# Values of three attentions written token by token to DRAM and read back, in place of a masked copy and transposes

## What is computed

```
q, k, v = split(x @ qkv_w.T + qkv_b)          # x: 64 images, 17 tokens, 192 features
q, k = rms_norm(q), rms_norm(k)                # first block's attention (a0) only
w = softmax(q @ k.T / sqrt(16))                # per image and head: 17 x 17
ctx = w @ v                                    # 12 heads of 16 features
h = h + ctx @ proj_w.T + proj_b
```

## Time and profile before

| | us |
|---|---|
| median of 3 runs | 935.1 |
| lowest and highest run | 934.97, 940.88 |
| profiled execution, its own time | 934.18 |
| span of the profiled execution | 932.1 |
| stage a0, from TensorE's first to last instruction | about 39.5 to 145.7 |
| stage a2 | about 553.7 to 636.2 |
| stage a3 | about 727.2 to 838.4 |

### The profile page before, as it was taken

How to read it: one execution, slowest core, us unless ns; L and a number is a source line. 1 busy time by engine, 2 the same in 40 slices (tenths; PEclk the granted TensorE clock), 3 DMA queues, 4 the chain that set the end, 5 groups by cost and what they waited for, 6 DMA issues and landing times. The chain is left out here.

```text
span 932.1 us, 16890 instructions
## 1 busy us (share of the span) xinstructions
PE 854.9 (92%) x6194; PEld 608.5 (65%) x6195; DVE 447.4 (48%) x903; ACT 387.8 (42%) x857; POOL 186.7 (20%) x207
## 2 busy tenths in 40 slices
PE   6899888999998799999989789999999999999997
PEld 5556656677775467777668466765687566666776
DVE  5566676777744412222268666551104566633111
ACT  2366653453542022333243864554151455532332
POOL 0610003444500134445200012220000000002232
PEclk9999999999988899999999999999999999997999
DMA  8000000000004967112150019000000211102111
GB/s 294 1 2 1 1 2 0 1 2 1 1 2 102 256 182 198 46 51 46 39 164 3 0 45 258 6 2 28 1 1 1 56 50 50 52 19 97 43 51 34
DMA packets 30638, 51.07 MB, mean 55 GB/s; under 512 B 3750, under 2 KB 23752, under 8 KB 30572
## 3 DMA queue, kind: packets, MB, share of 16 engines
q1 hardware_dynamic: 22140, 36.09, 14.0%
q0 software_dynamic: 4416, 9.84, 3.8%
q10 hardware_dynamic: 4016, 4.23, 1.4%
HBM read 43.30 MB, written 6.83 MB: 54 GB/s over the span
## 5 line engine op out<-in xcount | busy, mean ns | idle before, releaser
L79 PE MATMUL banks<-con 128*128 128x512 f32 (+1 forms) x206 | 95.1, 572 | 3.0 <-DVEq L2136 1.4
L1846 PE MATMUL banks<-moe_wu,moe_xf 96*128 x256 | 92.1, 505 | 1.6 <-ACT moe_xf L1954 0.8
L634 PE MATMUL banks<-x,a_wqkv 96*96 96x272 f32 x288 | 74.6, 397 | 0.9 <-PEq L457 0.5
L1846 PEld LDWEIGHTS banks<-moe_wu,moe_xf 96*128 96x128 f32 x256 | 47.5, 195 | 31.4 <-issue 4.8
L944 ACT ACTIVATE a_vt<-banks 102x384 f32<-102x384 f32 x96 | 41.9, 488 | 50.4 <-PE banks L710 50.1
L154 ACT ACTIVATE ln_sq<-x 96x544 f32<-96x544 f32 x32 | 21.1, 658 | 93.2 <-DVE x L146 93.2
L634 PEld LDWEIGHTS banks<-x,a_wqkv 96*96 96x96 f32 x288 | 45.4, 164 | 18.2 <-issue 3.2
L79 PEld LDWEIGHTS banks<-con 128*128 128x128 f32 x206 | 38.4, 202 | 25.9 <-issue 22.4
L2151 DVE TENSOR_TENSOR moe_hid<-banks,moe_gs 128x384 f32<-128x384 f32 x32 | 17.9, 558 | 77.6 <-PE banks L1846 77.6
L710 PE MATMUL banks<-con,a_vx 96*102 96x96 f32 x384 | 42.7, 253 | 7.4 <-ACT a_vt L944 6.1
L2008 POOL DMA_INDIRECT moe_xs<-moe_x_rows,moe_taken x32 | 31.2, 974 | 76.1 <-PE banks L1830 54.2
(11 more groups left out here) (409 smaller groups left out, 1772.2 us busy)
## 6 DMA issues: line engine op xcount, KB each, us to landing
moe_wu<-in_moe_up SPq DMA_DIRECT2D x16, 576.0 KB, 8.9
f_w<-in_f_e SPq DMA_DIRECT2D x10, 576.0 KB, 14.6
moe_wd<-in_moe_down SPq DMA_DIRECT2D x16, 288.0 KB, 9.9
patch_px<-in_patches SPq DMA_DIRECT2D x4, 768.0 KB, 9.4
f_wu<-in_f_up SPq DMA_DIRECT2D x4, 582.0 KB
f_wd<-in_f_down SPq DMA_DIRECT2D x4, 576.0 KB
f_x_rows<-f_xtok ACTq DMA_DIRECT2D x4, 384.0 KB, 3.4
a_wqkv<-in_a_wqkv SPq DMA_DIRECT2D x3, 432.0 KB, 8.3
```

Source lines behind the costliest of these rows:

```text
L79: self.nc.tensor.matmul(self.ps[bank][:, 0:width], self.ident, self.con[:, 0:width], start=True, stop=True)
L634: last = nc.tensor.matmul(ps[2 + m][0:HD, 0:CW], wqkv[:, a, j * D + m * HD:j * D + (m + 1) * HD], chunk(x, c)[:, a], start=a == 0, stop=a ...
L1846: last = nc.tensor.matmul(ps[2 + 2 * p + u][:, 0:BW], xf[0:KU[a], p, a], wu[0:KU[a], bass.ds(e, 1), a, u * BW:(u + 1) * BW].rearrange("p e ...
```

## The change

The values no longer go through the masked copy and the transposes. TensorE projects them token-major (`values`): the tokens are the stationary operand, so that a result has tokens on partitions: two groups of products for 128 tokens by 192 features, and one of the last 32 tokens of the chunk for each half. ScalarE evicts them in two instructions (`take_values`) into `vtok`. SP writes them to DRAM in four transfers (`write_values`) as two planes, one for each half, of 272 rows of 96 features. Then six transfers for each chunk (`read_heads`) read them back, one for each head in a half: 18 partitions (17 keys and one of padding), 32 runs in each (16 images in 2 planes) of 16 features, that is 64 bytes. They land in `vt`, which GpSimd has set to zero before (`vt_zero`), on partitions key * 6 + head. So the order of the 102 columns becomes (key, head) where it was (head, key): `kx`, `p`, the maxima and the sums follow it. `vt` is double by chunk.

For chunk 0, SP issues the reads of heads 0, 2 and 4 and ScalarE those of 1, 3 and 5; for the others SP issues all six. The read of chunk c waits until the writes of its chunk have landed, and from chunk 2 on for the products that still read the buffer. `values` of chunks 0 and 1 run in the stage's opening, those of chunk 2 and 3 at the head of the loop for chunks 0 and 1. The weights loaded ahead are cut in four parts (`load_part`), one issued after each chunk's reads.

```diff
-    def load(self, sp):
-        sp.dma_start(self.gw[:], self.dram["gw"]).then_inc(self.gw_in, 16)
-        for i in range(6):
+    def load_part(self, sp, part):
+        if part == 0:
+            sp.dma_start(self.gw[:], self.dram["gw"]).then_inc(self.gw_in, 16)
+        for i in self.PARTS[part]:
...
+    def load_part(self, sp, part):
+        self.load(sp, range(part, part + 1))
...
+        vtok = sb("vtok", [128, 2, 2 * D + HD])
+        vt_rows = sb("vt", [(N + 1) * HH, 2, 2 * IC, HD])
+        v_rows = nc.dram_tensor(name + "_v_rows", (NC, 2 * CW + 1, HD), F32).ap()
...
+        def read_heads(eng, c, heads):
+            for h in heads:
+                eng.dma_start(vt_rows[h::HH, c % 2, :, h * HW:(h + 1) * HW],
+                              bass.AP(v_rows.tensor, c * (2 * CW + 1) * HD + h * HW, [[HD, N + 1], [N * HD, 2 * IC], [1, HW]])).then_inc(v_in[c % 2], 16)
...
-            for w in ahead:
-                w.load(sp)
+            def write_values(c):
+                rows = v_rows[c, 0:2 * CW].rearrange("(a t) d -> t a d", a=2)
+                for u in range(2):
+                    sp.wait_ge(v_taken, 2 * c + 1)
+                    sp.dma_start(rows[128 * u:128 * (u + 1)], vtok[:, c % 2, u * D:(u + 1) * D].rearrange("p (a d) -> p a d", a=2)).then_inc(v_written, 16)
+                for a in range(2):
+                    sp.wait_ge(v_taken, 2 * c + 2)
+                    sp.dma_start(rows[256:CW, a], vtok[SLOT * (a + 1) - (CW - 256):SLOT * (a + 1), c % 2, 2 * D:2 * D + HD]).then_inc(v_written, 16)
+            def read_values(c):
+                sp.wait_ge(v_written, 64 * (c + 1))
+                if c < 2:
+                    sp.wait_ge(vt_zero, c + 1)
+                else:
+                    sp.wait_ge(ctx_ready, GPC * (c - 1))
+                read_heads(sp, c, range(HH) if c else range(0, HH, 2))
+            sp.wait_ge(vt_zero, 1)
+            sp.dma_start(v_rows[:, 2 * CW:2 * CW + 1].rearrange("c t d -> t c d"), vt_rows[0:1, 0, 0:NC]).then_inc(v_padded, 16)
+            write_values(0)
+            sp.wait_ge(v_padded, 16)
+            read_values(0)
+            for c in range(NC):
+                if c + 1 < NC:
+                    write_values(c + 1)
+                    read_values(c + 1)
+                for w in ahead:
+                    w.load_part(sp, c)
...
-            def project_v(c, m):
-                pe.wait_ge(qk_evicted, NT * c + 2 + m + 1)
-                project(c, 2, v_proj, m)
+            def values(c):
+                if c >= 1:
+                    pe.wait_ge(v_taken, 2 * c)
+                for u in range(2):
+                    for a in range(2):
+                        tokens = chunk(x, c)[:, a, 128 * u:128 * (u + 1)]
+                        nc.tensor.matmul(v_bank[:, u * D:(u + 1) * D], tokens, wqkv[:, a, 2 * D:3 * D], start=a == 0, stop=a == 1)
+                for a in range(2):
+                    tokens = chunk(x, c)[:, a, CW - SLOT:CW]
+                    for m in range(2):
+                        last = nc.tensor.matmul(v_bank[SLOT * m:SLOT * (m + 1), 2 * D:2 * D + HD], tokens,
+                                                wqkv[:, a, 2 * D + m * HD:2 * D + (m + 1) * HD], start=a == 0, stop=a == 1)
+                last.then_inc(v_proj, 1)
...
             def weigh(g):
+                c = g // GPC
                 pe.wait_ge(pt_evicted, g + 1)
-                pe.wait_ge(vt_evicted, (g + 1) * FV)
+                if g % GPC == 0:
+                    pe.wait_ge(v_in[c % 2], 16 * HH * (c // 2 + 1))
...
+            def take_values(c):
+                act.wait_ge(v_proj, c + 1)
+                if c >= 2:
+                    act.wait_ge(v_written, 64 * (c - 1))
+                nc.scalar.activation(vtok[:, c % 2, 0:2 * D], v_bank[:, 0:2 * D], ACT.Copy).then_inc(v_taken, 1)
+                nc.scalar.activation(vtok[0:64, c % 2, 2 * D:2 * D + HD], v_bank[0:64, 2 * D:2 * D + HD], ACT.Copy).then_inc(v_taken, 1)
...
+            act.wait_ge(v_written, 64)
+            act.wait_ge(v_padded, 16)
+            act.wait_ge(vt_zero, 1)
+            read_heads(act, 0, range(1, HH, 2))
...
+            for c in range(2):
+                pool.memset(vt_rows[:, c], 0.0).then_inc(vt_zero, 1)
+                if c == 0 and response is not None:
+                    response.on_pool(pool, 1)
```

More of the change, by code:

```diff
@@ L280, in allocate @@
             self.bg, self.b2 = self.sb("bg", [128, E]), self.sb("b2", [128, E, D])
+    def load_part(self, sp, part):
+        if part == 0:
+            self.load(sp)
     def load(self, sp):
@@ L647, in project_q @@
                     project(c, 0, q_proj, m)
-            def project_v(c, m):
-                pe.wait_ge(qk_evicted, NT * c + 2 + m + 1)
-                project(c, 2, v_proj, m)
+            def values(c):
+                if c in carried:
+                    pe.wait_ge(before.ready, c + 1)
+                if c >= 1:
[10 more added lines that the diff above has]
+                last.then_inc(v_proj, 1)
             def states():
@@ L695, in scores, with turn_inputs @@
                 last.then_inc(scored, 1)
[L697 to L721 removed]
+            def turn_inputs(g):
+                if g == 0:
+                    pe.wait_ge(s_taken, 1)
+                else:
+                    pe.wait_ge(xt_taken, g)
+                for f in range(2):
+                    for a in range(2):
+                        o = (g * GI + 4 * f) * N
+                        last = nc.tensor.transpose(ps[6][0:4 * N, (2 * f + a) * HD:(2 * f + a + 1) * HD],
+                                                   x[:, a, o:o + 4 * N], env.ident[0:HD, 0:HD])
+                last.then_inc(xt_ready, 1)
             def turn_weights(g):
@@ L747, in weigh @@
                                                 pt[:, g % 2, 2 * (i // 4) + a, SLOT * (i % 4):SLOT * (i % 4 + 1)],
-                                                vt[:, g % 2, i, a, :], start=True, stop=True)
+                                                vt[:, c % 2, a, (g % GPC) * GI + i, :], start=True, stop=True)
                 last.then_inc(ctx_ready, 1)
@@ L799, in _ @@
                 pe.wait_ge(wo_in, 32)
+            values(0)
+            if quantum:
                 states()
             project_k(0)
+            values(1)
             for c in carried:
@@ L812, in _ @@
                 head_mean_square(1)
-            for m in range(2):
-                project_v(0, m)
             if rms:
@@ L823, in _ @@
                 more = c + 1 < NC
-                turn_values(2 * c)
+                if quantum:
+                    if c == 0:
+                        pe.wait_ge(s_factor, 1)
+                    turn_inputs(2 * c)
+                if c + 2 < NC:
+                    values(c + 2)
                 if c >= 1:
@@ L857, in _ @@
                     head_mean_square(NT * (c + 1) + 3)
-                if more:
-                    project_v(c + 1, 0)
                 if quantum:
```

145 lines of the change are left out of this document (57 added, 88 removed).

## The result

| | before | after |
|---|---|---|
| median, us | 935.04 | 975.76 |
| lowest and highest run | 934.89, 940.88 | 971.3, 981.56 |
| span of the profiled execution | 932.1 | 969.0 |

What follows compares the result with a forecast made beforehand. TensorE was taken to bound all three attention stages, with SyncE's queue ending a3 after the change. 934.2 - 5.2 - 8.1 + 2.3 + 7.0 = 930.2, with 0.9 to the median: 931 us; range 912 to 950.

Steps and rivals of the forecast that it cites:

- by the same count as above: a0's boundaries, counted like a2's with measured piece lengths kept in the new order: -2.2, -3.1 and -1.9 us.
- a2's -8.1: Stage a2: periods of 16.8 or 15.7 us for 18.68, plus 0.3 us from the opening; 8.1 us shorter.
- a0's -5.2: Stage a0: opening longer, three boundaries shorter without transposes and VectorE's copy; 5.2 us shorter, bounds -2 to -8.
- The opening was forecast at +2.05: a0's opening: values of two chunks before the first scores, few transposes taken out; 2.05 us longer.
- a3's +2.3: End of a3: SyncE's queue with the experts' weights ends after TensorE, hiding its gain; stage 2.3 us longer.
- TensorE alone was forecast at -14.5: a3: TensorE's list shortens by 1.3 in the opening and 3.5, 5 and 5 at boundaries, ending near 824 us.
- SyncE was forecast done 113.6 us into the stage: a3: SyncE issues its last expert weights about 841 us, by 828.3 + 21 r with r = 0.6.
- 17.0 were forecast on top: a3: the first weights are issued later by 11.6 + 9 r us, behind the first two chunks' writes and reads.
- the sum had 1 us: a3, SyncE's queue between weight parts: 1 us in each 1 + 6 r + 1.5 for chunks 2 and 3.
- r: Time of one read of 18 by 32 runs of 64 bytes: 0.6 us, low 0.45, up to 1.2, worst 1.6.
- Rival C: Slower, chance 0.20: reads cost r = 1.2 us, a3 +14.8 and f3 +8; total 945 us, 960 with r = 1.6.
- f3's +7.0: Start of f3: last up weights still occupy one engine, delaying token rows and the first gather; 7.0 us longer.

Runs made afterwards that it cites:

- the stall away: Changed kernel with a2's scaling of x on VectorE moved behind the scaling of the second group's context; 965.5 us, a2 74.3 us.
- the filled and cut version: Changed kernel with idle products sized to the gap, a2's scaling of x late and up weights in transfers of 96 and 1 partitions; 923.9 us, 0.9872 times before.
- the clock held: Changed kernel with a2's scaling late, up weights cut and later chunks' value products moved into the gap as real work; 917.2 us, 0.9787 times before.

## Why the prediction was wrong

By stages the forecast was -5.2, -8.1, +2.3 and +7.0 for a0, a2, a3 and f3, and 0 for the rest; measured were +10.6, -0.3, +13.0, +10.1 and +3.5.

- **The step that failed: the clock had no term in the sum, and a0 and a3 were counted "by the same count as above", from a2.** That count lets the second set of context transposes follow the first after 1.46 or 1.42 us. For a2 it holds (1.45 with the stall away). In a0 the distance was VectorE's chain already before, 3.39, 4.02 and 4.02 us, and in a3 2.91, 3.54 and 3.54. There the half projection did not lengthen TensorE's list but covered a wait. Without it the wait grew from 0.97 to 2.19 and from 1.60 to 2.82 us in a0 and from 0.88 to 2.16 in a3, and behind it the clock was at its lower level for 7 to 20 us. The clock was read from the earlier trace rows (0.98 and 1.00) and taken to stay; no term, no rival and no bound had it, though the 0.98 of a0 was a fall behind such a wait. That the gap brings the fall was shown in both directions, by filling it in the changed kernel and by opening it in the kernel before, though not every gap brings one. Against the filled and cut version a0 lost about 11 us by gap and clock (117.3 and 106.1).
- **The order (key, head).** The prediction asked only whether the copy of the keys gets slower. It took 6.04 us for 6.47, but that is not the new order: with the same order it took 6.51 where VectorE's scaling began in its first half. The sum over strided columns, 0.3 us slower, was never priced. With VectorE's stall and the clock behind it, it took all of a2's gain.
- **a2's -8.1** was right otherwise: -8.5 with the stall away, with periods of 16.8 and 15.7 us as forecast.
- **a0's -5.2.** The opening was forecast at +2.05 and measured at +6.5, of which 2.8 are left at the full clock and in a better order (18.5 against 15.7). With the clock held a0 gains 9.5 (97.2), more than forecast.
- **a3's +2.3**: measured +13.0. TensorE alone was forecast at -14.5 (its terms give 14.8); measured are -9.4 with both limits gone. SyncE was forecast done 113.6 us into the stage; measured are 121.0. Of the 7.4 between, 5.2 arose ahead of the first weights, which were issued 23.3 us into the stage (at 764.45; before, it was 1.1, and 17.0 were forecast on top), and 2.2 between the parts. The read of 0.79 us for 0.6 explains 1.7 of the first and 2.3 of the second; the other 3.5 lie in the first two chunks' writes, their landing and the router's loads. So the writes of the values that took 12.4 and 15.4 us behind the weights, where the sum had 1 us, made the last values late, but not the queue's end: the weights needed that time anyway, as the sum had it. A packet of 64 bytes took 10.8 ns for 9, which is 0.39 us for a read on 16 engines and 0.69 on 9; the issue of 0.79 us is longer than either, so it was probably the issue that set r, but no run varied it. Rival C had the right sign and the wrong mechanism.
- **f3's +7.0**: right in its mechanism. The gather came at 23.3 us against 22.8 forecast, and at 15.3 with the transfer cut. The stage lost 10.1: about 7.2 by the late tokens, and 2.6 by the low clock behind TensorE's idle time of 9.3 us.
- **The sum's form.** Each part was subtracted or added as if independent. In a3 two limits ended within 3.4 us of one another, and the second one was hidden.

## What to carry to other kernels

Before you take work off an engine that bounds a stage, ask of each wait that the work covered how long it will be without it, in each stage and not in one for all: waits of 2.2 to 2.8 us in place of 0.9 to 1.6 were followed by 7 to 20 us at half the clock. Work that is moved should fill such a gap and not open one, and an order on VectorE beside GpSimd is worth a look at the tenth of a microsecond. Where two limits are equally long, test them together: in a3 neither cure was worth 3 us alone, and both 22.

## What the runs showed of the hardware that I had not expected

- The clock falls behind some gaps of TensorE and not behind others of the same length. Kernel before, a0: waits of 0.97 and 1.60 us left it at 1.00, and a second one of 1.60 was followed by 3 us at 0.50. Changed kernel: of eight gaps of 2.2 to 2.8 us seven were followed by 0.50, and a2's second (2.17 us) was not. The kernel before with the projection moved: gaps of 1.89 and 2.53 us left the clock at 1.00, and the third (2.52, to 122.9) was followed by 0.50. What decides between them stays open. The same kernel can enter a stage at either level.
- A multiplication of VectorE with both inputs in SBUF took 0.72 us alone, 0.9 where GpSimd's second copy began after it, 3.6 where that copy (3.0 us) had just begun, and 1.6 where it was in its last microsecond.
- A sum over 17 columns took 0.57 us with adjacent columns and 0.86 with a stride of six.
- A transfer of 97 partitions holds up what is issued behind it on the same queue: a pair of writes of 96 KB took 12.4 and 15.4 us to issue, and 1.1 to 1.4 with the 97 cut into 96 and 1.
